# A scan in place of a two-step threshold, second layer-norm statistics on ScalarE, and one filler matmul fewer, in a windowed-attention block with two layer norms

## The reference

```python
h = _layernorm(x) * (1 + ca) + sa
# per head, for each token t over the 64 tokens of its window:
dist = jnp.sqrt((diff * diff * m_h).sum(axis=-1) + 1e-08)
neg_d, loc = jax.lax.top_k(-dist, K)          # the 32 nearest
infl = jnp.exp(-topd)
infl = infl / (infl.sum(axis=-1, keepdims=True) + 1e-08)
context = jnp.einsum('btk,btkd->btd', infl, neighbor_v)
...
x = x + ga * (out_sparse @ decoder)
h = _layernorm(x) * (1 + cb) + sb              # the second layer norm
x = x + gb * (h + weighted experts of h)
```

## Time and profile before

| | before |
|---|---|
| median of 3 runs | 736.17 us (735.36 to 737.92) |
| profiled execution: its time, its span | 735.44 us, 733.6 us |
| busy share of the span: PE, DVE, ACT, POOL | 88%, 90%, 70%, 70% |
| mean granted clock of PE | 0.937 of full |

### The profile page before, as it was taken

The page is one execution under the profiler, slowest core; times in us unless marked ns, Lnnn a source line. Parts: engine busy times, 40 slices in busy tenths (PEclk is TensorE's granted clock), DMA queues, the critical chain, the costliest instruction groups (busy, mean ns, idle before and its releaser), DMA issues. The chain is left out here.

```text
span 733.6 us, 22908 instructions
## 1 busy us (share of the span) xinstructions
PE 642.7 (88%) x6133; PEld 442.2 (60%) x6133; DVE 660.3 (90%) x5082; ACT 511.2 (70%) x1542; POOL 512.0 (70%) x811
## 2 busy tenths in 40 slices
PE   4987889899998999999999999999999999998785
PEld 2543446666666666666666666666666666666564
DVE  5874798999999999999999999999999999999920
ACT  2894136777777777777777777777777777777632
POOL 3012426888887888888888888888888888887651
PEclk9896587999999999999999999999999999999855
DMA  6210000000000000000000000000000000000000
GB/s 198 87 59 4 14 14 18 22 25 25 24 26 24 24 26 22 25 22 25 25 26 25 25 26 25 24 25 25 25 24 23 24 26 21 25 25 23 14 8 11
DMA packets 41184, 21.22 MB, mean 29 GB/s; under 512 B 6040, under 2 KB 40544, under 8 KB 41056
## 3 DMA queue, kind: packets, MB, share of 16 engines
q1 hardware_dynamic: 41056, 19.77, 9.4%
HBM read 10.44 MB, written 4.19 MB: 20 GB/s over the span
## 5 line engine op out<-in xcount | busy, mean ns | idle before, releaser
L987 DVE MAX8 gsgn_all<-modn_all 128x8 f32<-128x32 f32 x2048 | 206.7, 175 | 0.0
L556 POOL TENSOR_TENSOR big<-big,con 128x512 f32<-128x512 f32 x128 | 160.0, 1272 | 27.2 <-DVE big L1039 27.2
L993 DVE MATCH_REPLACE8 modn_all<-gsgn_all,modn_all 128x32 f32<-128x32 f32 x1024 | 166.5, 175 | 0.0
L1227 PE MATMUL psC<-vst,big 128*128 128x68 f32 x512 | 105.5, 289 | 49.4 <-POOL big L556 49.4
L1227 PEld LDWEIGHTS psC<-vst,big 128*128 128x128 f32 x512 | 80.5, 198 | 72.2 <-POOL big L556 71.1
L764 ACT ACTIVATE z_all<-psW,bias 128x512 f32<-128x512 f32 x64 | 44.0, 688 | 84.1 <-PE psW L1296 83.0
L1228 PE MATMUL psC<-vst,big 128*128 128x68 f32 x512 | 102.2, 282 | 0.0
L1228 PEld LDWEIGHTS psC<-vst,big 128*128 128x128 f32 x512 | 81.1, 200 | 0.0
L497 POOL TENSOR_TENSOR wmod_sb<-key,theta 128x512 f32<-128x512 f32 x64 | 67.2, 1050 | 17.7 <-DVE theta L1070 10.1
L993 DVE MATCH_VALUE_LOAD modn_all<-gsgn_all,modn_all 128x8 f32 x1024 | 78.8, 77 | 0.0
L542 POOL TENSOR_TENSOR t<-cst,rden 128x128 f32<-128x128 f32 x64 | 25.8, 403 | 63.7 <-DVE rden L1028 63.7
(11 more groups left out here) (212 smaller groups left out, 1640.1 us busy)
## 6 DMA issues: line engine op xcount, KB each, us to landing
tst<-qT_all SPq DMA_DIRECT2D x256, 17.0 KB
big<-in_x SPq DMA_DIRECT2D x16, 256.0 KB, 2.8
xs<-in_x SPq DMA_DIRECT2D x64, 64.0 KB, 1.9
out<-yo SPq DMA_DIRECT2D x64, 64.0 KB, 1.5
sst<-nst SPq DMA_DIRECT2D x128, 3.0 KB
tst<-nst SPq DMA_DIRECT2D x128, 2.0 KB
con<-in_consts SPq DMA_DIRECT2D x1, 581.5 KB, 6.0
wmod_sb<-in_wmod SPq DMA_DIRECT2D x1, 384.0 KB, 4.2
```

Source lines behind the costliest of these rows:

```text
L556: nc.gpsimd.tensor_tensor(wab[:, k % 2, v].rearrange("p (r t) -> p r t", r=4), wsel.rearrange("p (r t) -> p r t", r=4), part.unsqueeze(1). ...
L987: last = v.max(top[:, u, h, where], low_high[:, u, h])
L993: last = v.match_replace(low_high[:, u, h], top[:, u, h, 0:8], low_high[:, u, h], GONE)
L1227: mm(o, wab[:, k % 2, 0, cols], vst[:, blk + 1:blk + 3, r], start=True, stop=False)
```

## The change

Threshold. `top` and `meet` get buffers of their own with 17 places for each head. Place 0 of each head holds +1e30 for lows and -1e30 for highs, set once by two POOL memsets. One `tensor_tensor_scan` over the 136 flat elements then runs state = max(min(high, state), low); the sentinel at place 0 resets the state at the start of each head, and the last place of each head holds the threshold. It replaces "meet" and "theta". POOL's diff reads the threshold at place 16 of `meet`.

Statistics. ACT's copy of x2 also accumulates its row sum, a second ACT instruction scales it to the negated mean, a third squares the deviations and accumulates them, and Ln and Exp follow at once in the same step. The two DVE instructions and the block of three ACT instructions at the start of ACT's step go.

Fillers. `keep_clock` ahead of the transpose of `osp` issues two matmuls in place of three.

```diff
-        top = gsgn_all[:].rearrange("p u (h n) -> p u h n", h=NH)
-        meet = gabs_all[:, 0].rearrange("p (h n) -> p h n", h=NH)
-        theta = sb("theta", [P, 2, NH])
+        top = sb("top", [P, 2, NH, NT])
+        meet = sb("meet", [P, 2, NH, NT])
-        pHigh = psW[:, 1, 0:2 * NH * 8].rearrange("p (h n) -> p h n", h=NH)
+        pHigh = psW[:, 1, 0:NH * NT]
...
+            nc.gpsimd.memset(top[:, 0, :, 0], BIG).then_inc(top_set, 1)
+            nc.gpsimd.memset(top[:, 1, :, 0], -BIG).then_inc(top_set, 1)
...
-                                            theta[:, k % 2].unsqueeze(2).broadcast_to([P, NH, WIN]),
+                                            meet[:, k % 2, :, NT - 1:NT].broadcast_to([P, NH, WIN]),
...
-                k = i - 4
-                if there(k):
-                    s = k % 2
-                    act.wait_ge(mvc_ready, k + 1)
-                    need(act, nc_ready, k - 1)
-                    need(act, rs_done, k)
-                    nc.scalar.activation(lv_c[:], mv_c[:, s, 1:2], ACT.Ln, bias=bias[:, 0:1]).then_inc(lnc_done, 1)
-                    nc.scalar.activation(nm_c[:, s:s + 1], mv_c[:, s, 0:1], ACT.Copy, scale=-1.0).then_inc(nm_done, 1)
-                    act.wait_ge(lnc_done, k + 1)
-                    nc.scalar.activation(rs_c[:, s:s + 1], lv_c[:], ACT.Exp, scale=-0.5).then_inc(rs_done, 1)
...
                 k = i - 3
                 if there(k):
+                    s = k % 2
                     act.wait_ge(att_ready, k + 1)
                     need(act, y_ready, k - 1)
-                    nc.scalar.activation(x2[:, k % 2], pAtt, ACT.Copy).then_inc(x2_ready, 1)
+                    need(act, rs_done, k)
+                    nc.scalar.activation(x2[:, s], pAtt, ACT.Copy, accum_out=sum_c[:]).then_inc(x2_ready, 1)
+                    act.wait_ge(x2_ready, k + 1)
+                    nc.scalar.activation(nm_c[:, s:s + 1], sum_c[:], ACT.Copy, scale=-1.0 / D).then_inc(nm_done, 1)
+                    act.wait_ge(nm_done, k + 1)
+                    nc.scalar.activation(dev_c[:], x2[:, s], ACT.Square, bias=nm_c[:, s:s + 1],
+                                         accum_out=ssq_c[:]).then_inc(ssq_done, 1)
+                    act.wait_ge(ssq_done, k + 1)
+                    nc.scalar.activation(lv_c[:], ssq_c[:], ACT.Ln, bias=bias[:, 0:1], scale=1.0 / D).then_inc(lnc_done, 1)
+                    act.wait_ge(lnc_done, k + 1)
+                    nc.scalar.activation(rs_c[:, s:s + 1], lv_c[:], ACT.Exp, scale=-0.5).then_inc(rs_done, 1)
...
-                    v.bn_stats(st_c[:], x2[:, k % 2]).then_inc(stc_ready, 1)
...
-                    v.bn_aggr(mv_c[:, k % 2], st_c[:]).then_inc(mvc_ready, 1)
...
-                    v.tensor_scalar(pHigh, top[:, 1], -1.0, None, ALU.mult).then_inc(high_done, 1)
+                    if i == 0:
+                        dve.wait_ge(top_set, 2)
+                    v.tensor_scalar(pHigh, top[:, 1].rearrange("p h n -> p (h n)"), -1.0, None, ALU.mult).then_inc(high_done, 1)
                     dve.wait_ge(high_done, i + 1)
-                    v.scalar_tensor_tensor(out=meet, in0=pHigh, scalar=0.0, in1=top[:, 0], op0=ALU.max,
-                                           op1=ALU.max).then_inc(meet_done, 1)
-                    dve.wait_ge(meet_done, i + 1)
                     need(dve, diff_ready, i - 1)
-                    v.tensor_reduce(theta[:, i % 2], meet, AX_X, ALU.min).then_inc(theta_ready, 1)
+                    v.tensor_tensor_scan(meet[:, i % 2].rearrange("p h n -> p (h n)"), pHigh,
+                                         top[:, 0].rearrange("p h n -> p (h n)"), BIG, ALU.min, ALU.max).then_inc(theta_ready, 1)
...
-                    keep_clock(psX[:, 2 * P:4 * P], P, 3)
+                    keep_clock(psX[:, 2 * P:4 * P], P, 2)
```

More of the change, by code:

```diff
@@ L34 @@
 VP = 2 * VD
+NT = 17
 BIG = 1e30
@@ L208, in adaln_block @@
         x2 = sb("x2", [P, 2, D])
-        st_c = sb("st_c", [P, 6])
-        mv_c = sb("mv_c", [P, 2, 2])
+        sum_c = sb("sum_c", [P, 1])
+        dev_c = sb("dev_c", [P, D])
+        ssq_c = sb("ssq_c", [P, 1])
         lv_c = sb("lv_c", [P, 1])
@@ L311, in adaln_block @@
         picked = sem("picked")
+        top_set = sem("top_set")
         high_done = sem("high_done")
-        meet_done = sem("meet_done")
         theta_ready = sem("theta_ready")
@@ L339, in adaln_block @@
         x2_ready = sem("x2_ready")
-        stc_ready = sem("stc_ready")
-        mvc_ready = sem("mvc_ready")
+        ssq_done = sem("ssq_done")
         lnc_done = sem("lnc_done")
@@ L983, in pick @@
             def pick(rnd, u):
-                where = slice(8 * rnd, 8 * rnd + 8)
+                where = slice(8 * rnd + 1, 8 * rnd + 9)
                 for h in range(NH):
@@ L992, in drop @@
                 for h in range(NH):
-                    last = v.match_replace(low_high[:, u, h], top[:, u, h, 0:8], low_high[:, u, h], GONE)
+                    last = v.match_replace(low_high[:, u, h], top[:, u, h, 1:9], low_high[:, u, h], GONE)
                 last.then_inc(picked, 1)
@@ L1054, in step @@
                     pick(1, 1)
-                if there(k):
-                    dve.wait_ge(stc_ready, k + 1)
-                    need(dve, nc_ready, k - 1)
-                    v.bn_aggr(mv_c[:, k % 2], st_c[:]).then_inc(mvc_ready, 1)
                 if there(i):
```

## The result

The changed kernel takes 718.28 us (median of 4 runs, 716.72 to 722.14) against 736.56 us before (4 runs, 735.36 to 737.92). The ratio is 0.976, 95% interval 0.973 to 0.979: 18.3 us less. Forecast were 713 us, 703 to 720. A ratio is taken between launches within 1.5% of the fastest of their kernel; for the first four kernels of the experiments this leaves 5 of the 17 launches of the kernel before, with a mean of 730.3 us where the median of all 17 is 736.1, so that those four ratios lie nearer to 1 than the medians do. The profiled execution took 718.80 us, its span is 717.0 and PE's mean granted clock 0.947.

What follows compares the result with a forecast made beforehand. DVE was taken to bound the kernel. 20.9 us over 58 steps, 0.2 in steps 0 to 2 and 1.5 in the drain made 22.6 us saved, so 713 us, range 703 to 720.

Steps and rivals of the forecast that it cites:

- DVE bounds the kernel, so its sum sets the step: DVE's instructions pace the other engines; the sum of its savings takes the step from 9.47 to 9.11 us.
- 58 steps: DVE paces steps 3 to about 60, 58 of 64; at 0.36 us each this saves 20.9 us.
- bn_aggr worth nothing, bn_stats 0.19, meet 0.32: Savings per step in us from removing these DVE instructions; bn_aggr only fills time in which high waits for the last pick.
- The scan at 0.43: On DVE, the scan replacing theta's reduce (0.29 us) was to take 0.43 us, between ends of 0.30 and 0.50.
- meet at full rate: First rival's support: meet's two operations take 0.29 us; a full-rate scan (0.30) would give 705 us; chance 0.15.
- ACT's chain, 1.6 us: On ACT, the new statistics take about 1.6 us from x2's start until ACT is free, and fit the hole there.
- the sum per step of 0.36: DVE's saving per step: 0.19 + 0.32 - 0.01 - 0.14 = 0.36 us, from 9.47 to 9.11.
- The counts, infl and rden ... come from C: Inputs DVE waits for come from PE's C; its later start eats 0.36 of a reserve read as over 1 us.
- My fifth rival: The loop w to wab to C to the counts to w already runs at DVE's pace: 736 us; chance 0.03.
- The drain, 1.5 us: In the last steps, earlier statistics save PE's waiting, less some added waits and missing fillers: together 1.5 us saved.
- The fillers: On PE, removing one filler frees 0.14 to 0.19 us, covered by the idle ahead of C, so worth nothing itself.
- The rival's effect: Fourth rival: the removed filler held PE's clock, in the hole ahead of C; the kernel gets slower; chance 0.04.

Runs made afterwards that it cites:

- the first four kernels of the experiments: Scan alone, statistics alone (kernel before), den in PSUM, no den (changed kernel): ratios 0.992, 0.983, 0.974, 0.968.
- each part alone: The kernel before with only the scan (722.98 us), and with only the statistics on ACT (719.88 us).
- den is out of POOL's way: The changed kernel with den's output moved to PSUM (709.37 us), and with den and its 1e-8 left out (708.08 us).
- the part alone: The kernel before with only the statistics moved to ACT: 719.88 us, ratio 0.983.

## Why the prediction was right or wrong

- **DVE bounds the kernel, so its sum sets the step.** Right in the kernel before and in each part alone (9.31 and 9.27 against 9.30 and 9.28 by the sum), and right again once den is out of POOL's way (9.11 and 9.04). Wrong for the changed kernel itself: another loop closes at 9.28. None of the signs of being wrong that I had listed (idle in brackets, a clock under 1.00, a scan away from 0.43) showed; only the length of the step did. That it sets 58 steps was read from the kernel before, where PE waits 1.60 us for wab a last time at 691.23 and its clock falls to 0.50 a microsecond later.
- **bn_aggr worth nothing, bn_stats 0.19, meet 0.32.** Right: high starts 0.04 behind the last pick with or without bn_aggr, and the part alone gives 0.20.
- **The scan at 0.43.** Right, 0.44 in all 64. The 0.14 us in the sum, by which the scan was to be longer than the reduce, was my estimate: two slots of 0.99 ns for each of 136 elements on the fixed 0.163, between the two ends of 0.30 and 0.50. No run had shown it. The changed kernel showed 0.15 in its place (0.44 against 0.29), about 2.0 ns an element by the same sum; why an element takes two slots no run shows. The nearest row, meet at full rate, would have misled.
- **ACT's chain, 1.6 us.** Right, 1.59, and Square's 0.40 too. It fits: between 150 and 640 us DVE has no idle time in brackets.
- **The step that failed** is the sum per step of 0.36, and in it the tacit assumption that the DVE rows which the change leaves alone keep their durations. I noted that "diff starts about 0.2 later" on DVE's clock and that POOL "needs 9.47 - 1.29 = 8.2", and asked only whether POOL's queue fits into a step. I did not ask which DVE instruction would now run beside which POOL instruction. The later diff puts T 0.16 later, and T ends where den would run. den rose from 0.17 to 0.33, the step came to 9.28 and the steps gave 12.8 us (12.2 and 0.6) in place of 21.1. "The counts, infl and rden ... come from C" looked for the reserve in waits that show as idle time, and this wait does not show so. My fifth rival had a loop at DVE's pace, but another one, and bounding by all or nothing.
- **What holds den.** The experiments narrow it down: an SBUF-to-SBUF den of one input is held (0.33), one of two inputs too (0.32), a den that writes PSUM is not (0.18), d2 with one input in PSUM is not (0.68 to 0.70). What makes it wait for POOL, and whether it waits with its reading or with its writing, no run shows.
- **The drain, 1.5 us.** Behind the last C 1.7 were gained, close to what was reckoned, about 1.4 of it by the earlier statistics. 2.4 more came in the profiled execution because the clock fell from 1.00 to 0.50 later (6.5 us into the step and not 1 us), which no reasoning of mine had in it: luck. It made up for some of the loop's shortfall, so the total (18.3 for a forecast of 23) looks better than the reasoning was; that it lies within 703 to 720 is owed to the width of the range.
- **The fillers.** Right that one is worth nothing (steps of 9.27 with three and 9.28 with two, the clock 1.00 in both). The rival's effect begins only below what was changed (1.00 with one, 0.93 with none).

## What to carry to other kernels

When a change moves two engines against each other by a few tenths, list what will run beside what: here VectorE's den was held until a multiplication on GpSimd ended, and the wait stood in its duration (0.33 us in place of 0.17), not in front of it. A short instruction whose end follows another engine's end by the same few hundredths in two kernels (here 0.02 to 0.03 us), at different lengths, is probably waiting; moving its output or its place tells. And test a bound by adding work: an additional instruction that costs nothing on an engine that is 98% busy (one more MAX8 of 0.09 us, the step at 9.28 with and without it) says that the engine's work is not the bound.

## What the runs showed of the hardware

- A scan with min and max over 128x136 fp32, one input in PSUM, takes 0.44 us; a reduction over 128x128 took 0.29.
- An 8-column SBUF-to-SBUF instruction of DVE ended 0.01 to 0.04 us after POOL's 0.40 us multiplication in nearly every step of the nine kernels that have it in its old place, at lengths of 0.17, 0.19, 0.23, 0.32 and 0.33; behind the cut, clear of POOL, it took 0.17. MAX8 and high (to PSUM) took 1.58 and 0.29 with POOL idle and 1.57 and 0.30 beside POOL's wab. The reductions took 0.69 beside POOL's diff, and the scan (one input in PSUM) 0.44 beside wab.
- Reading an accumulated sum on ACT is an instruction of its own, 0.19 to 0.20 us. The next dependent one starts 0.02 to 0.03 us behind its end, 0.12 behind the end of the instruction whose sum it reads.
- PE's granted clock stayed at 1.00 with holes of up to 0.87 us in each step of 9.26, and fell at times (0.88 to 0.97 over stretches of 50 us) with holes of 1.23.
